# Queries of two attentions projected straight into turned form, with their root moved into the exponential's scale

## The reference

```python
q = rms_norm(y @ Wq + bq, gq).reshape(b, -1, 16, 16)        # y = layernorm(x)
k = rms_norm(ctx @ Wk_img + bk_img, gk_img).reshape(b, -1, 16, 16)
v = (ctx @ Wv_img + bv_img).reshape(b, -1, 16, 16)
p = softmax(einsum('bqnd,bknd->bnqk', q, k) / 4)
x = x + tanh(g_xattn) * (einsum('bnqk,bknd->bqnd', p, v).reshape(b, -1, 256) @ Wo + bo)
# rms_norm(z, g) = z * rsqrt(mean(z * z) + 1e-6) * g, the mean over all 256 channels
```

## Time and profile before

| | |
|---|---|
| median of 3 runs | 3711.77 us (3710.74 to 3715.72) |
| the profiled execution, its own time | 3704.24 us |
| its span, from the first to the last instruction | 3702.5 us |
| busy: PE / PEld / DVE / ACT / POOL | 78% / 49% / 60% / 40% / 29% of the span |
| attention of layer 2, first load to last update of x | 2075.8 to 2289.0 us |
| attention of layer 3, first load | 2695.6 us |
| keys and values, first load | 704.0 us |

### The profile page before, as it was taken

One profiled execution on the slowest core, in us unless ns is written; L12 is line 12 of the kernel. 1 busy time (PEld: TensorE's weight loads), 2 busy tenths in 40 slices (PEclk: granted clock), 3 DMA queues, 4 the chain that ended last, 5 costly groups with the idle time before them and its releaser, 6 DMA issues. The chain is left out here.

```text
span 3702.5 us, 59792 instructions
## 1 busy us (share of the span) xinstructions
PE 2874.9 (78%) x19922; PEld 1817.1 (49%) x19922; DVE 2234.3 (60%) x5017; ACT 1493.3 (40%) x3096; POOL 1066.7 (29%) x1424
## 2 busy tenths in 40 slices
PE   5388884476699994559947698999979749999993
PEld 4233333332355553423323476444557638888782
DVE  7689993687577775734468697888869720000003
ACT  5267772155122224559935454222245311111110
POOL 3111110277133335412279432000033351111110
PEclk7599996699899997579968899999989759999996
DMA  8766643299422223388500242000044221111204
GB/s 267 173 115 120 119 107 137 95 372 361 146 81 80 80 79 135 126 132 123 102 1 1 104 158 64 1 1 1 1 129 139 94 71 58 47 54 50 85 28 136
DMA packets 261320, 386.33 MB, mean 104 GB/s; under 512 B 56321, under 2 KB 188654, under 8 KB 260768
## 3 DMA queue, kind: packets, MB, share of 16 engines
q1 hardware_dynamic: 234192, 312.76, 31.4%
q0 software_dynamic: 25152, 68.22, 5.3%
q10 hardware_dynamic: 1680, 1.57, 0.2%
HBM read 227.75 MB, written 160.24 MB: 105 GB/s over the span
## 5 line engine op out<-in xcount | busy, mean ns | idle before, releaser
L3120 POOL DMA_INDIRECT rows_out<-e_out,e_tr_dest x224 | 234.6, 1047 | 874.9 <-DVE e_out L3750 511.8
L1195 ACT ACTIVATE a_pt<-a_psS 128x512 f32<-128x512 f32 x512 | 277.6, 595 | 156.2 <-PE a_psS L1093 151.9
L3750 DVE COPY e_out<-e_psD 128x512 f32<-128x512 f32 x40 | 27.7, 692 | 494.0 <-PE e_psD L3718 493.9
L1217 DVE TENSOR_REDUCE a_mx_sb<-a_psM 128x4 f32<-128x1024 f32 x256 | 292.9, 1213 | 18.9 <-PE a_psM L1076 17.7
L3518 PE MATMUL e_psG<-e_wgu,e_yT 128*128 x576 | 274.9, 600 | 26.9 <-ACT e_yT L3546 24.3
L1107 PE MATMUL a_psV<-a_pt,a_vt 128*18 128x256 f32 x4096 | 293.6, 389 | 1.3 <-issue 0.8
L3718 PE MATMUL e_psD<-e_w,e_hT 128*128 128x256 f32 x1280 | 291.5, 387 | 0.0
L3707 PE MATMUL e_psH<-e_yT,e_w 128*128 128x256 f32 x1280 | 285.2, 381 | 1.6 <-issue 0.8
L3650 ACT ACTIVATE e_hT<-e_psH 128x512 f32<-128x512 f32 x160 | 95.5, 597 | 454.6 <-PE e_psH L3707 454.6
L3718 PEld LDWEIGHTS e_psD<-e_w,e_hT 128*128 128x128 f32 x1280 | 246.9, 195 | 33.7
L3707 PEld LDWEIGHTS e_psH<-e_yT,e_w 128*128 128x128 f32 x1280 | 244.7, 191 | 35.7 <-issue 2.1
(11 more groups left out here) (427 smaller groups left out, 6137.7 us busy)
## 6 DMA issues: line engine op xcount, KB each, us to landing
kbd<-e_bgu SPq DMA_DIRECT2D x64, 512.0 KB, 4.5
cr_kbd<-kbd SPq DMA_DIRECT2D x64, 512.0 KB, 3.4
rows_in<-zeros POOLq DMA_DIRECT2D x36, 522.0 KB, 6.2
e_xin<-rows_in SPq DMA_DIRECT2D x144, 128.0 KB
vbd<-e_bd SPq DMA_DIRECT2D x64, 272.0 KB, 4.6
cr_vbd<-vbd SPq DMA_DIRECT2D x64, 272.0 KB, 2.7
cq_rows<-rows_out SPq DMA_DIRECT2D x32, 512.0 KB, 5.8
e_w<-in_L_ffn_w_dram SPq DMA_DIRECT2D x16, 1024.0 KB, 7.6
```

Of the source, the lines that this page charges most:

```text
L1195: act.activation(pt[:, probs(t, h), b, :, :], psS[:, unit(t, h, b) % S_BANKS, :].rearrange("p (k c) -> p k c", k=KC), ACT.Exp, scale=scale ...
L1217: dve.tensor_reduce(mx[:, t % 2, :, h, :], psM[:, k % 2, :, :].rearrange("p b (f c) -> p b f c", f=2), AX_X, ALU.max).then_inc(ring_read, 1)
L3120: pool.indirect_dma_start(out=self.rows_out[0:limit, :], out_offset=bass.IndirectOffsetOnAxis(ap=self.dest[:, t:t + 1], axis=0), in_=rows, ...
```

## The change

The queries are projected with the weights as the stationary and yT as the moving operand, so that they come out turned, channels on the partitions; four matmuls over 128 columns (eight records) take the place of two over 256 (four records). The bias is then one value per partition and is loaded as two columns (`bias_q`). The turning of queries, its copy and the normalising on VectorE are gone; the biased, unnormalised queries go into the scores, and `qT` has three buffers. ScalarE squares them (no sum), Pool adds the two halves of 128 channels (`sqsum`), and TensorE sums over the partitions with a matmul against a column of ones (`sum_squares`, in the place of `turn_q`). ScalarE copies the resulting column, Pool takes the root one step later than before, with the factor for 1/4 inside, and the exponential uses it as a scale for each token. The gain of the queries is multiplied into the gain of the keys, once, in the keys' phase, which loads two more rows for it.

```diff
@@ KeysValues.sync_start
             sp.dma_start(self.gain[:, layer, :], gk.rearrange("(a n) -> a n", a=1).broadcast_to([P, DIM])).then_inc(self.w_loaded, 16)
+            sp.dma_start(self.query_gain[:, layer, :], gq.rearrange("(a n) -> a n", a=1).broadcast_to([P, DIM])).then_inc(self.w_loaded, 16)
@@ KeysValues.tensor, and vector_setup
-        pe.wait_ge(self.w_loaded, 16 * 10)
+        pe.wait_ge(self.w_loaded, 16 * 12)
...
-        dve.wait_ge(self.w_loaded, 16 * 10)
+        dve.wait_ge(self.w_loaded, 16 * 12)
+        dve.tensor_tensor(self.gain, self.gain, self.query_gain, ALU.mult).then_inc(self.gained, 1)
         dve.wait_ge(self.made, 10)
+        dve.wait_ge(self.gained, 1)
@@ phase_cross, sync
-                for m, v in enumerate((bq, gq, bo)):
-                    sp.dma_start(gains[:, m, :], v.rearrange("(a n) -> a n", a=1).broadcast_to([P, DIM])).then_inc(w_loaded, 16)
+                for k in range(KC):
+                    sp.dma_start(bias_q[:, k:k + 1], bq[k * P:(k + 1) * P].rearrange("(p a) -> p a", a=1)).then_inc(w_loaded, 16)
+                sp.dma_start(bias_out[:, :], bo.rearrange("(a n) -> a n", a=1).broadcast_to([P, DIM])).then_inc(w_loaded, 16)
@@ gpsimd
+                pool.memset(ones[:, :], 1.0).then_inc(ones_made, 1)
...
                     t = s + 3
                     if ok(t):
                         pool.wait_ge(q_squared, t + 1)
-                        pool.tensor_scalar(base[:, t:t + 1], square[:, t:t + 1], 1.0 / DIM, 1e-6, ALU.mult, ALU.add).then_inc(q_based, 1)
+                        if t >= 2:
+                            pool.wait_ge(q_summed, t - 1)
+                        pool.tensor_tensor(sqsum[:, t % 2, :], sqT[:, t % 2, 0, :], sqT[:, t % 2, 1, :], ALU.add).then_inc(q_added, 1)
+                    t = s + 2
+                    if ok(t):
+                        pool.wait_ge(sum_copied, t + 1)
+                        pool.tensor_scalar(base[:, t:t + 1], square[:, t:t + 1], CW / DIM, CW * 1e-6, ALU.mult, ALU.add).then_inc(q_based, 1)
                         pool.wait_ge(q_based, t + 1)
                         pool.tensor_tensor(rms[:, t:t + 1], base[:, t:t + 1], core.half[:, 0:1], ALU.pow).then_inc(q_rooted, 1)
@@ tensor
                     if t >= 3:
-                        pe.wait_ge(q_copied, t - 2)
+                        pe.wait_ge(sum_copied, t - 2)
...
-                    for k in range(KC):
-                        ins = pe.matmul(psQ[:, 0, :], yT[:, u, k, :], wqs[:, k, :], start=(k == 0), stop=(k == KC - 1))
+                    for c in range(KC):
+                        for k in range(KC):
+                            ins = pe.matmul(psQ[:, 0, c * P:(c + 1) * P], wqs[:, k, c * P:(c + 1) * P], yT[:, u, k, :], start=(k == 0), stop=(k == KC - 1))
                     ins.then_inc(q_done, 1)
...
-                def turn_q(t):
+                def sum_squares(t):
                     u = t % 2
-                    pe.wait_ge(q_normed, t + 1)
+                    if t == 0:
+                        pe.wait_ge(ones_made, 1)
+                    pe.wait_ge(q_added, t + 1)
                     pe.wait_ge(y_copied, min(t + 3, TILES))
                     if t:
-                        pe.wait_ge(q_copied, t)
-                    for k in range(KC):
-                        ins = pe.transpose(psT[:, 1, k * P:(k + 1) * P], qn[:, u, k * P:(k + 1) * P], core.ident[:, :])
-                    ins.then_inc(q_turned, 1)
+                        pe.wait_ge(sum_copied, t)
+                    pe.matmul(psT[:, 1, 0:1], sqsum[:, u, :], ones[:, :], start=True, stop=True).then_inc(q_summed, 1)
 
                 def scores(t):
-                    u, m = t % 2, t % NK
-                    pe.wait_ge(q_copied, t + 1)
+                    u, m = t % 3, t % NK
+                    pe.wait_ge(q_ready, t + 1)
@@ scalar
                         act.wait_ge(shifted, t + 1)
-                        act.activation(prob[:, t % 2, :, :], prob[:, t % 2, :, :], ACT.Exp, scale=CW ** -0.5).then_inc(exped, 1)
+                        act.wait_ge(q_rooted, t + 1)
+                        act.activation(prob[:, t % 2, :, :], prob[:, t % 2, :, :], ACT.Exp, scale=rms[:, t:t + 1]).then_inc(exped, 1)
                     t = s + 3
                     if ok(t):
                         act.wait_ge(q_ready, t + 1)
-                        if t:
-                            act.wait_ge(q_squared, t)
-                        act.activation(junk[:, :], q[:, t % 2, :], ACT.Square, accum_out=square[:, t:t + 1]).then_inc(q_squared, 1)
+                        if t >= 2:
+                            act.wait_ge(q_added, t - 1)
+                        act.activation(sqT[:, t % 2, :, :], qT[:, t % 3, :, :], ACT.Square).then_inc(q_squared, 1)
                     t = s + 2
                     if ok(t):
-                        act.wait_ge(q_turned, t + 1)
-                        if t >= 2:
-                            for r in range(2):
-                                act.wait_ge(s_done[r], t - 1)
-                        act.activation(qT[:, t % 2, :, :], psT[:, 1, :].rearrange("p (k c) -> p k c", k=KC), ACT.Copy).then_inc(q_copied, 1)
+                        act.wait_ge(q_summed, t + 1)
+                        act.activation(square[:, t:t + 1], psT[:, 1, 0:1], ACT.Copy).then_inc(sum_copied, 1)
@@ vector
-                    if ok(s + 2):
-                        normalise(s + 2)
...
                         dve.wait_ge(q_done, t + 1)
-                        if t >= 2:
-                            dve.wait_ge(q_squared, t - 1)
-                            dve.wait_ge(q_normed, t - 1)
-                        dve.tensor_tensor(q[:, t % 2, :], psQ[:, 0, :], gains[:, 0, :], ALU.add).then_inc(q_ready, 1)
+                        if t >= 3:
+                            for r in range(2):
+                                dve.wait_ge(s_done[r], t - 2)
+                            dve.wait_ge(q_squared, t - 2)
+                        dve.tensor_tensor(qT[:, t % 3, :, :], psQ[:, 0, :].rearrange("p (k c) -> p k c", k=KC),
+                                          bias_q[:, :].rearrange("p (k a) -> p k a", a=1).broadcast_to([P, KC, P]), ALU.add).then_inc(q_ready, 1)
```

More of the change, by code:

```diff
@@ L1365, in sync_start @@
     def sync_start(self, sp):
-        for layer, (wk, wv, bk, bv, gk) in enumerate(self.weights):
+        for layer, (wk, wv, bk, bv, gk, gq) in enumerate(self.weights):
             for m, (ww, bb) in enumerate(((wk, bk), (wv, bv))):
@@ L1534, in phase_cross @@
     surveyed, averaged, eased, rooted, y_ready, y_turned, y_copied = (core.sem(n + k) for k in ("sv", "av", "es", "rt", "yr", "yt", "yc"))
[L1535 to L1536 removed]
+    q_done, q_ready, q_squared, q_added, q_summed, sum_copied, q_based, q_rooted, ones_made = (
+        core.sem(n + k) for k in ("qd", "qr", "qs", "qa", "qu", "uc", "qb", "qo", "om"))
     s_done = [core.sem(f"{n}sd{r}") for r in range(2)]
@@ L1546, in phase_cross @@
         wos = sb(ctx, n + "wo", [P, KC, DIM], F32)
-        gains = sb(ctx, n + "gains", [P, 3, DIM], F32)
+        bias_out = sb(ctx, n + "bo", [P, DIM], F32)
+        bias_q = sb(ctx, n + "bq", [P, KC], F32)
+        ones = sb(ctx, n + "ones", [P, 1], F32)
         kbd = sb(ctx, n + "kbd", [P, NK, KC, 2, CJ * SEQ], F32)
@@ L1622, in _ @@
                         pool.wait_ge(y_ready, t + 1)
-                        pool.tensor_tensor(core.xs[:, t, :], core.xs[:, t, :], gains[:, 2, :], ALU.add).then_inc(bias_added, 1)
+                        pool.tensor_tensor(core.xs[:, t, :], core.xs[:, t, :], bias_out[:, :], ALU.add).then_inc(bias_added, 1)
             @block.tensor
@@ L1780, in _ @@
             def _(dve):
-                def normalise(t):
-                    u = t % 2
-                    dve.wait_ge(q_rooted, t + 1)
-                    if t >= 2:
-                        dve.wait_ge(q_turned, t - 1)
-                    dve.scalar_tensor_tensor(out=qn[:, u, :], in0=q[:, u, :], scalar=rms[:, t:t + 1], in1=gains[:, 1, :],
-                                             op0=ALU.mult, op1=ALU.mult).then_inc(q_normed, 1)
                 dve.wait_ge(w_loaded, 16 * 5)
-                dve.tensor_scalar(gains[:, 2, :], gains[:, 2, :], gate, None, ALU.mult).then_inc(bias_scaled, 1)
+                dve.tensor_scalar(bias_out[:, :], bias_out[:, :], gate, None, ALU.mult).then_inc(bias_scaled, 1)
                 for s in range(-6, TILES + 4):
@@ L3765, in flamingo_decoder @@
     vbd = [dram(f"vbd{k}", [TILES, P, KeysValues.VBD]) for k in range(2)]
-    key_weights = (tuple(a["L2_xattn_" + k] for k in ("Wk_img", "Wv_img", "bk_img", "bv_img", "gk_img")),
-                   (turned[1], turned[2], *(a["L3_xattn_" + k] for k in ("b_k_img", "b_v_img", "g_k_img"))))
+    key_weights = (tuple(a["L2_xattn_" + k] for k in ("Wk_img", "Wv_img", "bk_img", "bv_img", "gk_img", "gq")),
+                   (turned[1], turned[2], *(a["L3_xattn_" + k] for k in ("b_k_img", "b_v_img", "g_k_img", "g_q"))))
```

(2 more changed lines are left out.)

18 lines of the change are left out of this document (8 added, 10 removed).

## The result

| | before | changed |
|---|---|---|
| median of 3 runs | 3711.77 us | 3688.6 us (3682.77 to 3691.23) |
| ratio, 95% interval | | 0.9926 [0.9910, 0.9942] |
| span of the profiled execution | 3702.5 us | 3689.2 us |
| attention of layer 2, first load to the next stage's first load | 214.25 us | 202.76 us |
| attention of layer 3, the same | 215.83 us | 203.10 us |

The medians are 23.2 us apart, 0.62%; the ratio in the table gives 0.74%, with an interval from 0.58 to 0.90% (22 to 33 us). 3694.0 was predicted. The two attentions alone are 11.5 and 12.7 us shorter, together 24.2. The two profiled spans differ by only 13.3, because two stretches that the attentions don't touch came out longer: keys and values 234.2 for 231.1 us, and layer 3's routing (first load of its router to the start of its experts' phase) 126.5 for 118.3.

The account below looks back on a forecast made before the run. A chain through the queries' root and normalising was taken as the bound, TensorE right behind. Per attention -3.8 - 5 - 0.6 = -9.4, twice -18.8, keys +1.0: -17.8, or 3694.0 us on the medians' scale; range 3680 to 3706.

Parts of the forecast that it names:

- The bound: Mid-attention before: a chain over maximum, exponential, square, root and normalising sets 5.83 us; TensorE's own work is 5.64.
- The middle: Steady tiles of each attention: period falls from 5.83 to 5.68 us, 3.8 us over 25 tiles.
- the router's price: Layer-2 router, same shape, four records in 0.52 us; so eight projection records cost at most 1.04 us.
- The rival with weight loads in the open: Query projection: weight loads of eight short records aren't hidden, period 6.29 us, total 3730 us; chance 0.06.
- The start: First tiles of each attention: scores no longer wait for turned queries; 5 us less, bounds 1 and 6.5.
- The walk of the maxima: Start of attention, step by step: first four maxima near 2094.8, 2098.4, 2102.5 and 2107.5, assuming the full clock.
- the five loads: Start of attention: still five, two now 4 bytes per partition instead of 128 KB, ahead of the output weights; no gain counted.
- the -18.8: Both attentions together: -9.4 us each from middle, start and end.
- The end: Last tiles of each attention, stepping at about 5.75 us before: 0.6 us less, bounds 0 and 1.5.
- Keys and values: Keys' phase: two more loads on SP's queue delay the first projection and context loads; +1.0 us, bounds 0 and 2.
- The rival in which only start and end gain: Attentions: another loop of about the old length holds the middle; -10 us in all, 3702 us; chance 0.16.
- The rival with more: Attentions: start at full clock, cheap ones matmul, projection at no price; 15 us per attention, 3683 us; chance 0.11.

Follow-up runs that it names:

- The exchange on Pool: Kernel before, with Pool's addition of the output bias to x moved ahead of its root of the queries; 3702.41 us, ratio 0.9978.
- the kernel with two turnings more: Kernel before, with TensorE's turning of the queries done twice for each tile; 3714.78 us, ratio 1.0001.

## Why the prediction was right

**The bound.** Right, and shown twice. The exchange on Pool takes the step to 5.64, which is 5.83 less the wait of 0.19. More work on TensorE costs nothing before and all of its price after.

**The middle.** Predicted 5.83 to 5.68 and 3.8 us per attention. Measured from the 5th to the 30th maximum of layer 2: 145.64 us before, 141.83 after, 3.81 less, a step of 5.673. The terms held: projection +0.03 (predicted +0.04, the router's price bounding it), matmul with ones 0.24 for 0.27, which the turned outputs take back with 0.25 for 0.22 (the prediction had taken 0.27 and 0.22), exponential +0.09 (0.2 taken, worth nothing), root done 6.67 us after the start of its step's scores (2163.37 to 2170.04, predicted 6.7).

**The rival with weight loads in the open** fell with the 0.99 us of eight records. Its price had a slip: eight at 0.19 us are 1.52, not 1.6, so that it stood for 3725, not 3730. The rule that it was set beside, from the Trainium skill, TensorE: Matmul & The Clock Gate, Part 3 (a weight load runs beside a matmul in flight only in other row groups), isn't borne out: all eight records use all 128 rows, and their loads lie beside the matmuls. The exponential with its scale from memory takes 1.15 us for 1.06. The Trainium skill, ScalarE: Activation LUTs, section "What ACT_TABLE_LOAD costs", gives about 93 ns for it, and the rows agree. ScalarE still idles 0.69 + 1.61 us a tile, so that it lengthens nothing.

**The start** was right in its mechanism and mis-sized. The walk of the maxima, counted from the first load (2075.8 before), put the maxima at 19.0, 22.6, 26.7 and 31.7 us; measured are 18.71, 22.59, 26.83 and 31.50. The fourth step was put at 5.3 and is 4.81. But the prediction then took 5 us rather than the walk's own difference, to leave room for a clock that falls back. In the changed kernel it didn't: the projection of 1.92 us at 2091.76 becomes 1.31 at 2096.22 and 1.06 from 2101.26 on. It had fallen back in the kernel before, at 2100 (granted 0.59, turned probabilities 1.92 us for 1.04), and that is gone as well. What it is worth can be read only roughly: the second step is 6.49 us there and 5.88 in the kernel with two turnings more, where the clock stayed up. Over the whole 30 us the granted clock is nearly the same, 0.72 for 0.71, since the changed kernel climbs later.

To the 5th maximum layer 2 gained 0.8 (first maximum) + 6.1 (four steps) = 6.9 us, layer 3 2.0 + 6.1 = 8.1. The first maximum holds a term that the prediction put at nothing, the five loads. VectorE's first statistics, which wait for the output weights, stand 7.43 us behind the first load for 7.97 in layer 2, and 8.09 for 9.49 in layer 3; so 0.5 of the 0.8 and 1.4 of the 2.0 come from this wait. In the profiled executions of the five kernels with three loads of 128 KB before the output weights it is 7.97 to 8.25 and 9.15 to 9.72 us in the two layers, in the three with one such load and two of 4 bytes per partition 7.43 to 8.35 and 6.83 to 8.09. That the smaller loads are the reason is likely, but no experiment has them alone. The start as a whole is 5.0 of the 5.4 us by which the two attentions did better than the -18.8.

**The end.** Predicted 0.6, measured 0.9: the last two steps are 5.45 and 4.56 us for 5.77 and 5.14 (layer 2).

**Keys and values.** Predicted +1.0 for two issues of 0.48; measured +1.4 to the first projection. What reaches the end is of the size of the spread of that stage, 2.4 us as the difference of the means with overlapping ranges, so this term is neither confirmed nor refuted.

**The sum** at the measured sizes is -24.2 for the attentions and 0 to +2.4 for the keys: 3687.6 to 3690.0 on the scale of the medians, beside 3688.6. On the scale of the profiled executions the same forecast was 3686.4, and the changed kernel's took 3691.23: there it is short by 4.8 us where in the medians it is over by 5.4. The difference is the spread of the other stages, the 118.3 us of layer 3's routing above all, so how near the total came says less than the terms do. The rival in which only start and end gain falls with the step of 5.67. The rival with more won named the right side: its 6.5 us for the start are near the measured 6.9 and 8.1, but the cheap records that it counted on in the middle weren't there.

## What to carry to other kernels

Where two engines look full, follow one item's period and ask of each instruction who released it; the bound is the loop that closes without a gap, and an extra instruction of known price put on the suspected engine settles it in one run. A value that enters a product only as a factor per row can be applied as late as the next instruction that has a scale of its own, and what that buys has two parts, in steady state and in the filling of the pipeline, which are priced apart (here 3.8 us, and 6.1 in the first four steps, of each attention). Give each load the semaphore of its first user: one counter for all loads of a stage had cost 7 us in each attention, more than the middle gained over 25 tiles.

## What was unexpected in the hardware

- A VectorE instruction over 256 elements that reads and writes SBUF took 0.94 us where it overlapped Pool's 0.72 us addition over 256 elements, and 0.48 where Pool was idle; in the kernel with two turnings more, where the overlap was down to 0.47 us in 12 tiles, it took 0.75. The maximum, which reads PSUM, isn't stretched by the same addition: 1.23 us at 2170.30 in the changed kernel. Who runs beside an instruction can double its price.
- Here a matmul in f32 with a single moving column isn't cheaper than one with 128: two records in 0.24 us, 0.22 for the second of two in a row, beside 0.99 / 8 = 0.12 for each record over 128 columns.
- ScalarE's copy of one column from PSUM to SBUF took 0.15 us, against 0.36 for 256 columns.
